# ScalarE copies the transposed rows of an expert block out of PSUM, in VectorE's place

## The reference, cut to what matters

```python
x = x + _layernorm(attn(_layernorm(x), Wq, bq, Wk, bk, Wv, bv, gamma))
x = x + _layernorm(ffn(_layernorm(x), W1, b1, W2, b2, gate_W, shared_W, shared_b, lng, lnb))

# ffn, with flat of shape (4096, 256):
probs = jax.nn.softmax(flat @ gate_W)
topk_w, topk_idx = jax.lax.top_k(probs, 2)            # and normalised: combine
out = 0.5 * gelu(flat @ shared_W + shared_b)
for e in range(8):
    h = gelu(flat @ W1[e] + b1[e])                    # 256 -> 1024
    out = out + combine[:, e:e + 1] * (h @ W2[e] + b2[e])   # 1024 -> 256
out = layernorm(out) * lng + lnb
```

## Time and profile before

| | |
|---|---|
| runs | 725.88, 727.56, 731.08 us; median 727.56 |
| span of the profiled execution | 729.0 us |
| its own time | the page gives its span alone: 1.4 us above the median of the runs |
| busy | PE 610.5 us (84%), DVE 465.5 (64%), ACT 445.1 (61%), POOL 318.4 (44%) |
| the chain that ended last | PE 69%, DVE 13%, issue 8%, ACT 4%, POOL 2% |
| the moved step, L1994 | 36 copies, 24.7 us busy, 687 ns each |

### The profile page before, as it was taken

The page is one execution under the profiler, slowest core; times in us unless marked ns, Lnnn a source line. Parts: engine busy times, 40 slices in busy tenths (PEclk is TensorE's granted clock), DMA queues, the critical chain, the costliest instruction groups (busy, mean ns, idle before and its releaser), DMA issues.

```text
span 729.0 us, 16808 instructions
## 1 busy us (share of the span) xinstructions
PE 610.5 (84%) x4903; PEld 517.1 (71%) x4903; DVE 465.5 (64%) x1242; ACT 445.1 (61%) x875; POOL 318.4 (44%) x435
## 2 busy tenths in 40 slices
PE   4778888798876898978979999999999999999600
PEld 3657677677655687866857877889898899888400
DVE  5479898899985554522447776644443544777884
ACT  2657767657744674633654686767567557578742
POOL 4000432535637322654662422245244367574684
PEclk9989999999997899988998999999999999999955
DMA  8553663551255321212111221122211129843466
GB/s 255 181 204 123 197 201 97 192 175 60 95 191 160 92 91 59 60 30 59 46 45 52 90 66 60 32 88 81 75 53 56 41 66 192 173 85 78 84 186 120
DMA packets 45272, 78.25 MB, mean 107 GB/s; under 512 B 16962, under 2 KB 30596, under 8 KB 44804
## 3 DMA queue, kind: packets, MB, share of 16 engines
q1 hardware_dynamic: 33492, 48.19, 20.7%
q0 software_dynamic: 11696, 28.98, 16.8%
HBM read 48.17 MB, written 28.98 MB: 106 GB/s over the span
## 4 chain that ended last, share of the span: by engine, by line
PE 69%; DVE 13%; issue 8%; ACT 4%; POOL 2%; another core or an unknown queue 1%; DMA 1%; DVEq 0%; ACTq 0%; POOLq 0%
PE banks L534 17%; PE banks L536 17%; PE banks L535 16%; PE banks L1022 3%; PE banks L957 3%; PE banks L1192 2%; PE banks L1090 2%; PE banks L980 2%; PE banks L976 2%; DVE W L1747 2%; PE banks L1005 1%; PE banks L1042 1%; DVE st L1601 1%; PE banks L1193 1%
## 5 line engine op out<-in xcount | busy, mean ns | idle before, releaser
L1514 ACT ACTIVATE X<-banks,b1T,tab 128x256 f32<-128x256 f32 x256 | 128.9, 553 | 125.0 <-PE banks L536 98.2
L1980 DVE SCALAR_TENSOR_TENSOR stage<-X,tab,stage 128x512 f16<-128x512 f32 (+1 forms) x160 | 108.7, 697 | 104.0 <-ACT stage L1520 76.3
L534 PE MATMUL banks<-W,stage 128*128 x576 | 160.8, 279 | 10.6 <-issue 7.2
L822 POOL DMA_INDIRECT y_rows<-X,tb x72 | 79.8, 1108 | 202.4 <-DVE X L2011 187.8
L536 PE MATMUL banks<-W,stage 128*128 x576 | 160.6, 279 | 4.3 <-issue 4.3
L535 PE MATMUL banks<-W,stage 128*128 x576 | 160.7, 279 | 2.8 <-issue 2.7
L534 PE MATMUL banks<-X,W 128*128 128x256 f16 x512 | 141.4, 276 | 10.2 <-DVE X L1994 7.9
L536 PE MATMUL banks<-X,W 128*128 128x256 f16 x512 | 141.0, 275 | 0.4 <-issue 0.4
L535 PE MATMUL banks<-X,W 128*128 128x256 f16 x512 | 141.2, 276 | 0.0
L1520 ACT ACTIVATE stage<-X,tab 128x512 f16<-128x512 f32 (+1 forms) x160 | 106.9, 677 | 10.7 <-ACT X L1514 6.9
L797 POOL DMA_INDIRECT table<-pay,slot_i x64 | 67.8, 1059 | 65.8 <-PE banks L1022 42.4
(11 more groups left out here) (300 smaller groups left out, 1155.1 us busy)
## 6 DMA issues: line engine op xcount, KB each, us to landing
stage<-in_L_ffn_W SPq DMA_DIRECT2D x10, 1024.0 KB
W<-in_L_ffn_W SPq DMA_DIRECT2D x6, 1024.0 KB, 8.6
X<-in_L_attn_x SPq DMA_DIRECT2D x8, 512.0 KB, 4.9
out<-X SPq DMA_DIRECT2D x8, 512.0 KB
xf_rows<-zone SPq DMA_DIRECT2D x8, 512.0 KB
u_rows<-b2b SPq DMA_DIRECT2D x8, 512.0 KB
X<-y_rows POOLq DMA_DIRECT2D x8, 512.0 KB
away<-W SPq DMA_DIRECT2D x1, 2048.0 KB, 7.4
```

The lines of the kernel that those rows point to most:

```text
L534: pe.matmul(o, lh, rh, start=first, stop=False)
L822: g.indirect_dma_start(out=y_rows, out_offset=bass.IndirectOffsetOnAxis(ap=tb[:, j % ROWS, h, 1:2], axis=0), in_=y32[:, j % 2 * HALVES + h ...
L1514: a.activation(tile, tile if joint(j) else PS[m][:, r * BT:(r + 1) * BT], ACT.Gelu, bias=b1T[:, bass.ds(e * NH + 2 * m + r, 1)], scale=tab ...
L1980: v.scalar_tensor_tensor(o[1], src, tab[:, 1, bass.ds(e, 1)], o[0], ALU.mult, ALU.subtract).then_inc(h_low, 1)
```

## The change

ACT takes over `turned_block` for block 0 and for blocks 4 to 35; blocks 1, 2 and 3 stay on DVE. On ACT the copy of block 0 stands after the square root for z (`spread(1, ...)`) and before that for x1; the copy of block j+1 stands after Gelu tile 2 of block j and before Gelu tile 3. DVE's splits then follow one another without the copy between them. The copy waits for the same semaphores as before (xb_turned, and h_ps of two blocks back).

```diff
+            def turned_block(j):
+                a.wait_ge(xb_turned, j + 1)
+                if j >= 2:
+                    a.wait_ge(h_ps, NH // 2 * (j - 1))
+                settle(a)
+                q = j % 2
+                a.activation(xbT[:, q * NF * 2:(q + 1) * NF * 2, :].rearrange("p a n -> p (a n)"), PS[4][:, :].bitcast(F16), ACT.Copy).then_inc(xb_ready, 1)
...
             spread(1, z_dev, (z_mean, T * B), 2, 1.0)
+            turned_block(0)
             spread(2, x1_dev, (x1_mean, T * B), 0, 1.0 / SX / SX)
...
             for j in range(3, NB):
-                gelu(j, 0, 4)
+                gelu(j, 0, 3)
+                if j + 1 < NB:
+                    turned_block(j + 1)
+                gelu(j, 3, 4)
                 lean_of(j)
...
             residual(B - 1)
-            turned_block(0)
             x1_stats(B - 1)
...
                     split(j, 1, 2)
-                    turned_block(j + 1)
                     add_parts(j, 3)
                     split(j, 2, 4)
                 else:
-                    split(j, 0, 2)
-                    if j + 1 < NB:
-                        turned_block(j + 1)
-                    split(j, 2, 4)
+                    split(j, 0, 4)
```

## The result

The changed kernel takes **733.54 us** (median of 14 runs, 727.80 to 740.51) against 727.47 us for the kernel before (14 runs beside it, 721.77 to 732.11): a ratio of **1.008**, 95% interval 1.0052 to 1.0108, some 6 us slower. That lies within the 1% that a measurement tells from no change. My forecast was 737.5; the range held the time, the likeliest class (slower by over 1%) did not come.

The account below looks back on a forecast made before the run. PE was taken to set the pace (69% of the chain that ended last). Terms 0.3 + 1.7 + 2.0 + 0.5 + 2.5 + 3.0 = 10.0 us, added to the median of 727.56, gave 737.5 us, range 727 to 742.

Parts of the forecast that it names:

- Ordinary blocks, 0: Ordinary blocks: ACT's copy ends later but before up() needs it, 3.6 us to spare on DVE; neither gain nor loss.
- Block 0, +0.3: Block 0: the held signal comes at 236.65 for ACT too, and its copy is 0.33 us longer; +0.3 us.
- my lower bound: Block 0: if only DVE was held, ACT copies from 233.07 and up(0) starts at 234.2 for 237.48; -3.2 us.
- Block 4, +1.7: Block 4: PE waits for ACT's copy, which stands behind tile 2, so up(4) starts at 289.7 for 287.98; +1.7 us.
- Blocks 13 to 16, +5.0: Joint blocks: ACT's copies delay DVE's sums; block 13 +2.0, block 11's held copy +0.5, blocks 14 to 16 +2.5 us.
- my two copies (2.0): Block 13: two ACT copies lie in the chain to DVE's first sum, for which PE waits; +2.0 us.
- Tail, +3.0: Blocks 32 to 35: a DVE and ACT chain passes one copy in each of blocks 32, 33 and 34; +3.0 us.
- Rival 1: Block 0 and block 11's copy: DVE alone was held, ACT is not; 733.5 us, within 1%, chance 0.25.
- Rival 2: Three stretches at clock 0.81: DVE's pending copy slows PE, so 19.8 us come back; 717.8 us, chance 0.10.
- Rival 3: Ordinary blocks: ACT's held copies come late for up(), 12 x 0.7 = 8 us; 745.5 us, chance 0.08.
- Rival 4: Block edges: unseen slack of DVE and ACT absorbs up to 8 of the 10 us; about 730 us, chance 0.12.

Follow-up runs that it names:

- D: Set of follow-up runs on one chip, which showed no holds: the change again and combinations, beside the kernel before, which took 692.32 us there.
- act_5_to_11: Kernel before with ACT copying only blocks 5 to 11, behind Gelu tile 2: ratio 1.002 to the kernel before.
- change_again: The changed kernel, unaltered, measured and profiled a second time beside the kernel before: 699.31 us, ratio 1.0085.
- A: Set of runs that measured the result: the changed kernel, 733.54 us, beside the kernel before, 727.47 us; ratio 1.008.
- C: Set of follow-up runs on one chip: ordinary copies, early copies and spread table writes, beside the kernel before, which took 737.25 us there.
- zero_and_ordinary: Kernel before with ACT copying block 0 and, behind Gelu tile 2, blocks 5 to 11 and 18 to 32: ratio 0.9919 to the kernel before.
- spread_table: Kernel before with GpSimd's last table writes moved apart into pairs, VectorE making all copies: ratio 0.9921 to the kernel before.
- only_block_4: Kernel before with ACT copying block 4 alone, behind Gelu tile 2 of block 3: ratio 1.0031 to the kernel before.

## Why the prediction was right in size and where it failed

- **Ordinary blocks, 0.** Right for blocks 18 to 31: PE 65.00 of 65 us, and 10.92 or 10.93 us for most blocks in every set, whoever copies (the fourteen take 153.0 to 155.3 us in sum, with no order by engine). Open for blocks 7 to 12, and wrong for block 12 on D, where PE waited 1.44 us for ACT's copy.
- **Block 0, +0.3.** The step that failed, in its form. I took the hold as a fact of the signal, with one end for both engines. With holds, four draws each way show no difference (mean 11.75 and 11.86 us from 0 to 1), but DVE was hardly held in two of its four. Without holds it was -3.26 us, as much as my lower bound, but by another way: 1.66 us of earlier start and 1.6 that go with the clock.
- **Block 4, +1.7.** The wait was right: 3.28 us for 1.53; +1.61 us on the chip without holds. Missed was the clock: with it the place cost 3.2 (the change) and 4.4 us (alone) on the others.
- **Blocks 13 to 16, +5.0.** Too large: 3.12 without holds, 1.8 to 2.8 with them, and 0.4 to 1.3 for blocks 13 to 17 alone. By block, without holds (12 to 13, and so on): +1.03, +0.24, +1.11, +0.33, +0.40. The +1.03 is up(12)'s wait for ACT's copy, not DVE's chain. The chain itself brought block 13's sum 1.68 us later, near my two copies (2.0); only 0.24 of it is left in the next interval, for 1.03 was already lost, and behind its longer wait act_5_to_11 had a clock of 0.76 (381 to 388 us; change_again 1.00 from 382 to 389). Behind it only block 14 passed on a whole copy; the slack that I read from single waits of 0.2 to 0.5 us was too small.
- **Tail, +3.0.** The path is right only in part, and what size it agrees in is luck. PE waits for ACT's copy before up(34), as forecast, but in neither profile of the change before up(35), and the loss is not one copy in each of three blocks. On D the transposes of blocks 32 to 34 keep their distance, 34 to 35 takes 4.17 us more, and all that follows 0.19 more. So the loss is that one wait, 2.56 us, and the clock behind it, some 1.7 (0.74 over 6.5 us). Of the wait, 0.9 us is the foreseen chain (ACT's tile 2 of block 33 starts 5.59 us behind block 34's transposes, in act_5_to_11 4.71); the rest is the copy's place. In sum 4.42 us without holds; with them 1.0 to 3.0 over the kernels that copy on DVE.
- **Sum.** 10.0 forecast, 6.1 measured in A and 7.0 in D (699.31 - 692.32). The places of D add up to 5.99 against act_5_to_11; the 4.0 us to the forecast are the joint blocks' 1.9 and block 0's 3.6, less the tail's 1.4. So the misses have different signs, and the sum missed by less than its terms together. By the medians the change is 5.0 us slower than act_5_to_11, and that one 2.0 slower than before; these 2.0 have no place. In A no sum by place gives the 6.1: the profiled execution of the change lies 5.7 us under its median, and blocks 7 to 12 alone take 7.9 us less in it than before.

Rival 1 gave 733.5 us, the measured time, and by its words it was wrong in A: ACT was held too, 16.7 us. It is the Trainium skill's rule ("SBUF — State Buffer", "Who interferes with whom": PE and ACT never wait on anyone), and the runs leave it untested: what was held is the start of a copy that waits for a signal of PE, while PE's own next instructions are late as well (waits of 1.0 to 1.2 us with "issue" as releaser), and at block 0 it ends where POOL's row of DMAs is taken away. PE is late too and D's same DMAs hold nobody, so it doesn't look like a port that one engine keeps from another; the cause of the hold stays open. Rival 2 counted three stretches; POOL writes the table in four rows, and in the kernel before the intervals beside them lost 6.9, 6.7, 3.1 and 7.0 us against 10.93. It had something: the loss beside POOL's rows of DMAs is real and can be removed (0.992 by spreading them), and on C's chip zero_and_ordinary gained the same. But DVE's pending copy is at most a part of its cause, for spread_table lost less with every copy on DVE; and in A it didn't decide. Rival 3 is refuted (its price of 0.7 us a copy came from no row). Rival 4 is in part what happened in the joint blocks.

Most of what the change lost, it lost because of where the copy stood: behind tile 2, in blocks (3, 11 on D, 33) in which ACT had been idle 4.2 to 6.8 us just before that tile. At blocks 4, 34 and 35 the same copies ahead of it are free or gain; at blocks 12, 33 and in the joint blocks the early place was not tried. The joint blocks' loss comes with the later last split: on D block 12's starts 1.68 us later behind block 12's transposes than in act_5_to_11 (378.52 - 356.69 for 377.62 - 357.47), and block 13's sum as much.

## What to carry to other kernels

What moving work to an engine with idle time gains or costs is decided by the position in its queue: put it where that engine already waits, not behind the instruction that ends the wait. Price each new wait of TensorE twice, once as time and once as the slow matmuls that may follow it. And before a "remote" hold enters a forecast, look whether another chip shows it at all.

## What the runs showed of the hardware

- **The holds differ from set to set.** Beside rows of GpSimd's indirect DMAs, four of them table writes, a block of 10.93 us took up to 17.96 in the kernel before and nothing more in D (54.63 us for five blocks against 71 to 83). The kernel before ran in 692 us there and in 727 to 737 elsewhere. One chip stands for each set, so chip and hour are not told apart.
- **Where they occur, copies that wait for TensorE start late on VectorE and on ScalarE:** DVE's after up to 7.66 us of idle time, ACT's after up to 2.92 at block 0 and 4.90 at block 4.
- **The clock** fell to the 1.2 GHz level behind waits of TensorE of 2.56, 2.76, 3.08, 3.17 and 3.28 us, and not behind 1.42, 1.57 and 2.34 us. In a joint block it fell behind a wait of 1.55 us (act_5_to_11, 0.76 from 381 to 388). A fall cost 1.5 us (up(4) in the change, 3.20 less 1.75 of waiting) to 2.8 us (only_block_4).
- ScalarE's copy of 128x1024 fp16 out of PSUM took 1.00 to 1.02 us in every kernel, VectorE's 0.68 to 0.69.
